# Drains on TensorE's queue behind its hand-overs in three stages of a graph network kernel

## The chip, the cores and the metric

The kernel runs on one core of a Trainium2 chip. A core has TensorE (matrix products into PSUM), VectorE, ScalarE, GpSimd and SyncE, each with an instruction queue of its own; they hand work to each other through semaphores, and DMA engines move data between HBM and the core's memories. The metric is the device time of one launch in microseconds. In the profile's rows PE is TensorE's matmuls, PEld its weight loads, PEldq its queue, DVE VectorE, ACT ScalarE, POOL GpSimd, SP SyncE.

## The reference

A graph has 3125 nodes with 32 features and 53125 edges, sorted by destination. Four layers follow each other, each on the normalised and rectified features, each added to them:

```python
h = maximum(layernorm(x), 0);  x = x + rel_layer(relu(rel_layer(h, V1, a1, ...)), V2, a2, ...)
h = maximum(layernorm(x), 0);  x = x + segment_sum(h[src], dst)                      # sum layer
h = maximum(layernorm(x), 0);  x = x + flow(h, edge_attr)                            # two edge MLPs, a node MLP
h = maximum(layernorm(x), 0);  x = attention(h) + x                                  # 4 heads of 8

def rel_layer(x, V, a, w_loop, bias):          # 20 edge types, 8 basis matrices
    W = einsum('rb,bio->rio', a, V)
    agg = segment_sum(x[src], dst * R + etypes).reshape(N, R, -1)
    return einsum('nri,rio->no', agg, W) + x @ w_loop + bias

def attention(x):
    scores = einsum('ehd,ehd->eh', q[dst], k[src]) * inv_sqrt_d
    e = exp(scores - segment_max(scores, dst)[dst])
    return (segment_sum(e[:, :, None] * v[src], dst) / segment_sum(e, dst)) @ Wo
```

## The kernel before

The edges are laid out in 440 tiles of 128, so that all edges of a tile have their destinations in one block of 128 nodes (25 blocks). A sum over the edges of a node is a matmul: the weights are a one-hot matrix of the tile's destinations (edges by nodes of the block), the moving operand is the tile's messages, and the result is added in PSUM to the block's columns. Which columns is data: TensorE reads the tiles' column offsets into registers first (`load_aligned`, line 84, and `load_columns`, line 1778).

The value of a source node comes to its edge in one of two ways. GpSimd gathers rows from a table in HBM, one indirect DMA for each tile (line 732 in the relational layers, 1038 in the sum layer, 1655 in attention). Or TensorE picks it from the node table that stands in SBUF: VectorE compares the tile's source numbers with the node numbers (`which`, lines 795 and 1073), and 25 matmuls, one for each block of nodes, add up the picked rows (lines 870 and 1126).

The stages follow each other; each is a block in which every engine has its own program, and the engines meet only through semaphores. The loops that concern us are written out in full, group after group. The order on TensorE is the order of the calls:

- Relational layers (two, 40 groups of 11 tiles each; 8 tiles gathered, 3 picked). For each group g: `pick(g)`, `gathered_messages(g)`, `coefficients(g)` (the type's 8 coefficients for the picked edges), `picked_messages(g-2)`, `basis_products(g)`. ScalarE takes the pick out of PSUM (line 844, waits for `pick_done`) and hands it back for the basis products; VectorE makes the one-hots (lines 782, 795, 804), weighs the basis products with the coefficients and adds them (812, 821). GpSimd may run 6 groups ahead and waits for `rows_used`, which `gathered_messages` gives.
- Sum layer (40 groups of 11 tiles, 7 gathered, 4 picked). For each group: `pick(g+1)`, `turn(g)` (transposes of the picked rows), `picked_rows(g-1)`, `gathered_rows(g)`. ScalarE copies between them (1100, 1104).
- Attention (55 groups of 8 tiles, in a pipeline of four steps). One step of TensorE has pieces of four groups: for tiles 0 to 3 `masked_scores`, each followed by two tiles of `pick_q` of the next group (and once by `pick_maxima` of the group before), for tiles 4 to 7 `masked_scores` with `turn_onehots` in between, then `add_up`, `turn_parts` and `load_columns`. VectorE takes each tile's maximum as its scores are done (1691), ScalarE turns and masks (1731, 1733, 1739).

Every such piece ends in the same way: the last matmul carries the update of the semaphore that another engine waits for, as in `pick` of the relational layers.

```python
for c in range(NB):
    last = pe.matmul(pp[g % 2][0:3 * F, 0:RW], hs[:, c].rearrange("p k f -> p (k f)"),
                     which[g % 2][:, c, :], start=(c == 0), stop=(c == NB - 1))
last.then_inc(pick_done, 1)
```

The flow stage between sum layer and attention, the sorting and the tables ahead of the layers are written likewise.

Of the kernel before, what the change touches and what calls it, by code (L numbers as in the profile page):

```python
# [679 lines left out]
def add_up_pass(nc, a, s, d, sb, ps, sem, k, init, finish):  # L680
# [4 lines left out]
    with ExitStack() as st:  # L685
        acc = ps(st, f"{name}_acc", [P, 2 * BANK])
        parts = init(st, acc)
        with ExitStack() as st1:
# [28 lines left out]
            with nc.Block() as block:  # L717
# [134 lines left out]
                def _(pe):  # L852
# [11 lines left out]
                    def pick(g):  # L864
                        load_aligned(pe, unused, regs[g % 3], s["dcol"][0:1, 0, :], g * RG)
                        pe.wait_ge(which_ready, g + 1)
                        if g >= 2:
                            pe.wait_ge(pick_taken, g - 1)
                        for c in range(NB):
                            last = pe.matmul(pp[g % 2][0:3 * F, 0:RW], hs[:, c].rearrange("p k f -> p (k f)"),  # L870
                                             which[g % 2][:, c, :], start=(c == 0), stop=(c == NB - 1))
                        last.then_inc(pick_done, 1)

                    def gathered_messages(g):
                        b = g % RBUFS
                        pe.wait_ge(hot_ready, g + 1)
                        pe.wait_ge(gathered[b], 16 * RGT * (g // RBUFS) + 16 * RGT)
                        for t in range(RGT):
                            last = add(g, t, rows[b][:, t, :])
                        last.then_inc(rows_used, 1)  # L880

                    def coefficients(g):
                        pe.wait_ge(kinds_ready, g + 1)
                        if g >= 1:
                            pe.wait_ge(coef_taken, g)
                        for t in range(RPT):
                            last = pe.matmul(pc[:, t * NBASIS:(t + 1) * NBASIS], kinds[g % 2][:, t * P:(t + 1) * P],
                                             ab[:], start=True, stop=True)
                        last.then_inc(coef_done, 1)

                    def basis_products(g):
# [3 lines left out]
                        for t in range(RPT):  # L895
                            for j in range(3):
                                last = pe.matmul(pz[:, t * NBASIS * F:(t + 1) * NBASIS * F],  # L897
                                                 gT[g % 2][:, t * P:(t + 1) * P], top(V[:])[:, j, :],
                                                 start=(j == 0), stop=(j == 2))
                        last.then_inc(z_done, 1)  # L900

                    def picked_messages(g):
                        pe.wait_ge(hot_ready, g + 1)
                        pe.wait_ge(msg_ready, g + 1)
                        for t in range(RPT):
                            last = add(g, RGT + t, msg[g % 2][:, t, :])
                        last.then_inc(used, 1)

                    for g in range(RGROUPS):
# [89 lines left out]
def sum_layer(nc, a, s, d, sb, ps, sem, more):  # L999
# [7 lines left out]
    with ExitStack() as st:  # L1007
# [5 lines left out]
        with ExitStack() as st2:  # L1013
# [16 lines left out]
            with nc.Block() as block:  # L1030
# [76 lines left out]
                def _(pe):  # L1107
# [12 lines left out]
                    def pick(g):  # L1120
# [4 lines left out]
                        for c in range(NB):  # L1125
                            last = pe.matmul(pp[g % 2][0:3 * F, 0:PT * P], hs[:, c].rearrange("p k f -> p (k f)"),  # L1126
                                             which[g % 2][:, c, :], start=(c == 0), stop=(c == NB - 1))
                        last.then_inc(pick_done, 1)

                    def gathered_rows(g):  # L1130
# [3 lines left out]
                        for t in range(GT):  # L1134
                            last = add(g, t, hot[b][:, t, :], [rows[b][:, t, :]])
                        last.then_inc(rows_used, 1)

                    def turn(g):
# [3 lines left out]
                        for t in range(PT):  # L1142
                            last = pe.transpose(pt[:, t * 3 * F:(t + 1) * 3 * F], turned[g % 2][:, t * P:(t + 1) * P],
                                                s["identb"][0:3 * F, 0:3 * F])
                        last.then_inc(turn_done, 1)

                    def picked_rows(g):
                        pe.wait_ge(hot_ready, g + 1)
                        pe.wait_ge(turn_taken, g + 1)
                        for t in range(PT):  # L1150
                            last = add(g, GT + t, hotb[g % bufs][:, t, :],
                                       [picked[g % 2][:, (3 * t + k) * F:(3 * t + k + 1) * F] for k in range(3)])
                        last.then_inc(used, 1)

                    groups = rounds * bufs
# [376 lines left out]
def attention_layer(nc, a, s, d, out, sb, ps, sem):  # L1532


    with ExitStack() as st:
# [81 lines left out]
        with ExitStack() as st2:  # L1617
# [29 lines left out]
            with nc.Block() as block:  # L1647
# [119 lines left out]
                def _(pe):  # L1767
                    regs = [pe.alloc_register(f"att_col{t}") for t in range(G)]

                    def turn_onehots(i, g, b):  # L1770
                        pe.wait_ge(hot_ready, g + 1)
                        for t in range(G):
                            last = pe.transpose(pOT[:, t * P:(t + 1) * P], hot[b][:, t, :], s["identb"][:])
                        last.then_inc(ot_done, 1)

                    def load_columns(i, g, b):
# [3 lines left out]
                    def pick_q(i, g, b, tiles):  # L1780
# [7 lines left out]
                        if tiles[-1] == G - 1:  # L1788
                            last.then_inc(q_done, 1)

                    def turn_parts(i, g, b):
                        pe.wait_ge(parts_ready, g + 1)
                        pe.sem_inc(go_pe, 1)
                        pe.transpose(pP[0:3 * G * HEADS, 0:P], top(sc[b][:].rearrange("p k t h -> p (k t h)")),
                                     s["identb"][:]).then_inc(parts_turned, 1)

                    def masked_scores(i, g, b, t):

                        if t == 0:
# [5 lines left out]
                        pe.matmul(r, pick[:, t, :], partT[b][:], start=False, stop=True, skip_group_check=True)\  # L1805
                            .then_inc(score_done, 1)

                    def pick_maxima(i, g, b):
                        pe.wait_ge(tparts_ready, g + 1)
                        pe.wait_ge(o_copied, g + 1)  # L1810
                        for t in range(G):
                            last = pe.matmul(pO[:, t * 3 * HEADS:(t + 1) * 3 * HEADS], OT[b][:, t, :],
                                             top(tm[b][:])[:, :, t, :], start=True, stop=True)
                        last.then_inc(rows_done, 1)

                    def add_up(i, g, b):
                        pe.wait_ge(mparts_ready, g + 1)
                        for t in range(G):
                            for k in range(3):
                                last = pe.matmul(pO[:, t * OW:(t + 1) * OW], hot[b][:, t, :], top(msg[b][:])[:, k, t, :],  # L1820
                                                 start=(k == 0), stop=(k == 2))
                        last.then_inc(o_done, 1)

                    pe.sem_inc(o_done, BUFS)
# [137 lines left out]
```

## Time and profile before

| | |
|---|---|
| median of 3 runs | 3510.46 us (3508.48 to 3511.75) |
| span of the profiled execution | 4186.2 us |
| mean granted clock of TensorE | 0.746 |
| busy share of the span: TensorE | 65% |
| VectorE | 63% |
| GpSimd | 56% |
| ScalarE | 13% |
| stages that the change touches (profiled) | relational 722 to 1240 and 1275 to 1800, sum 1830 to 2290, attention 3190 to 4095 us |
| flow stage (profiled) | 2330 to 3125 us |

The times in the rows are from one execution under the profiler, whose span is longer than the timed runs' median; the two are not mixed below without saying so. A matmul's end is modelled, its start is recorded. "Idle before" names what ended an engine's wait: another engine's line, "issue" where the profile shows nothing that it waited for, and "remote" where a semaphore update came that isn't traced to an instruction. The granted clock is a share of full speed.

### The profile page before, as it was taken

The numbers are of one execution on the slowest core, as the hardware profiler recorded it, in microseconds if no ns is written. First come the engines' busy times: TensorE is split into PE (matmuls) and PEld (weight loads), VectorE is DVE, ScalarE is ACT, GpSimd is POOL, SyncE is SP. The second block draws the span as 40 slices with busy tenths as digits, with TensorE's granted clock in tenths as the row PEclk, the third lists the DMA queues.
The fourth block names the chain that finished last, engine by engine and source line by source line (L and its number), as shares of the span: only waits on it lengthen the run. The fifth ranks groups of instructions, "written<-read, shape, count | busy, mean of one in ns | idle before, by whom it ended". The sixth has DMA issues, their size and how long they took to land. (4 is left out here: it accounts for less than half of the span.)

```text
span 4186.2 us, 55154 instructions
## 1 busy us (share of the span) xinstructions
PE 2723.7 (65%) x18509; PEld 1820.0 (43%) x18619; DVE 2656.6 (63%) x8007; ACT 533.4 (13%) x1242; POOL 2327.0 (56%) x2253
## 2 busy tenths in 40 slices
PE   0221001898895888957886899999994555555551
PEld 0100001676663676735554566666652222222221
DVE  9001002888854888868887688888854666665667
ACT  0000000000010000000100222222211222222220
POOL 3777774666606666446664566666725444444430
PEclk9555555777765777778887899999985667676665
DMA  5111002111111111111111000000000000000010
GB/s 88 39 37 26 7 7 62 21 21 21 19 62 38 21 22 22 13 22 23 24 24 16 10 10 10 11 10 11 11 4 21 16 17 17 17 17 16 18 14 4
DMA packets 125021, 91.49 MB, mean 22 GB/s; under 512 B 59542, under 2 KB 110678, under 8 KB 124118
## 3 DMA queue, kind: packets, MB, share of 16 engines
q0 software_dynamic: 70912, 41.10, 7.4%
q1 hardware_dynamic: 53846, 46.89, 4.7%
q8 instruction: 164, 2.69, 0.3%
q14 instruction: 99, 0.81, 0.1%
HBM read 60.42 MB, written 27.41 MB: 21 GB/s over the span
## 5 line engine op out<-in xcount | busy, mean ns | idle before, releaser
L732 POOL DMA_INDIRECT rel_rows<-message_table,message_indices x640 | 647.7, 1012 | 449.7 <-issue 173.8
L1287 POOL DMA_INDIRECT flow_x<-node_table,src_indices x440 | 524.9, 1193 | 293.4 <-PE p_x_turned L1406 153.7
L1655 POOL DMA_INDIRECT att_kv_rows<-kv_table,att_index x440 | 417.5, 949 | 474.4 <-DVE att_index L1666 342.7
L795 DVE TENSOR_SCALAR rel_source_onehot<-rel_sources,node_numbers 128x384 bf16<-128x384 f16 x2000 | 547.4, 321 | 208.3 <-remote 174.1
L393 POOL DMA_INDIRECT sorted_edges<-stage,sorted_row x416 | 429.6, 1033 | 191.7 <-issue 126.3
L1429 PE MATMUL flow_acc_bwd<-flow_onehot_j,flow_by_q 128*128 128x309 bf16 (+1 forms) x2530 | 516.9, 335 | 7.1 <-issue 0.2
L870 PE MATMUL p_rel_picked<-rel_source_onehot,rel_h_parts 128*96 128x384 bf16 x2000 | 458.4, 400 | 33.7 <-issue 24.6
L1691 DVE TENSOR_REDUCE att_tile_max<-p_att_scores 128x4 f32<-128x512 f32 x440 | 292.2, 688 | 236.6 <-PE p_att_scores L1805 166.9
L1038 POOL DMA_INDIRECT sum_rows<-node_table,src_indices x280 | 277.5, 991 | 220.5 <-issue 75.0
L870 PEld LDWEIGHTS p_rel_picked<-rel_source_onehot,rel_h_parts 128*96 128x96 bf16 x2000 | 309.2, 155 | 176.6 <-issue 33.3
L1073 DVE TENSOR_SCALAR sum_source_onehot<-sum_sources,node_numbers 128x512 bf16<-128x512 f16 x1000 | 309.1, 377 | 24.8 <-remote 24.8
L1803 PE MATMUL p_att_scores<-att_mask,identb 128*128 128x512 bf16 x440 | 235.6, 536 | 131.6 <-ACT att_parts_turned L1739 131.6
L1126 PE MATMUL p_sum_picked<-sum_source_onehot,sum_h_stack 128*96 128x512 bf16 x1000 | 271.5, 435 | 74.0 <-issue 51.6
L782 DVE TENSOR_TENSOR rel_onehot<-p_rel_lanes,dst_in_block 128x128 f32<-128x128 f32 x880 | 256.1, 291 | 15.7 <-issue 15.7
L1805 PE MATMUL p_att_scores<-att_parts_turned,att_pick 96*128 96x512 bf16 x440 | 241.7, 549 | 0.0
L1426 PE MATMUL flow_acc_fwd<-flow_messages,flow_onehot 128*128 128x32 bf16 x1320 | 235.4, 178 | 0.0
L624 PE MATMUL p_message<-w_rel,h_transposed 32*128 32x320 f32 x200 | 113.5, 744 | 186.8 <-issue 183.0
L1126 PEld LDWEIGHTS p_sum_picked<-sum_source_onehot,sum_h_stack 128*96 128x96 bf16 x1000 | 136.8, 141 | 195.2 <-issue 108.1
L601 DVE COPY message_rows<-p_message 128x320 f32<-128x320 f32 x50 | 24.6, 493 | 292.8 <-remote 227.0
L1341 DVE TENSOR_TENSOR flow_by_q<-flow_messages,source_q_mask 128x512 bf16<-128x512 bf16 x330 | 207.6, 684 | 0.0
L844 ACT CAST rel_picked<-p_rel_picked 96x384 bf16<-96x384 f32 x80 | 38.1, 476 | 1285.4 <-remote 851.6
L897 PE MATMUL p_rel_terms<-rel_basis_parts,rel_picked 96*128 96x256 bf16 x720 | 149.5, 378 | 74.4 <-issue 59.7
(287 smaller groups left out, 4502.7 us busy)
## 6 DMA issues: line engine op xcount, KB each, us to landing
message_table<-message_rows SPq DMA_DIRECT2D x50, 320.0 KB, 2.1
rel_rows<-message_table,message_indices POOLq DMA_INDIRECT x640
rel_sources<-source_rows SPq DMA_DIRECT2D x80, 96.0 KB
flow_x<-node_table,src_indices POOLq DMA_INDIRECT x440
att_kv_rows<-kv_table,att_index POOLq DMA_INDIRECT x440
sorted_edges<-stage,sorted_row POOLq DMA_INDIRECT x416
sum_sources<-source_rows SPq DMA_DIRECT2D x40, 128.0 KB
sum_rows<-node_table,src_indices POOLq DMA_INDIRECT x280
```

Of the source, the lines that this page charges most:

```text
L393: pool.indirect_dma_start(out=d["sorted"], out_offset=bass.IndirectOffsetOnAxis(ap=row[:, c:c + 1], axis=0), in_=stage[:, c, :], in_offset ...
L732: pool.indirect_dma_start(out=rows[b][:, t, :], out_offset=None, in_=d["messages"], in_offset=bass.IndirectOffsetOnAxis(ap=s["idx_msg"][:, ...
L782: last = dve.tensor_tensor(hot[b][:, lo:hi, :], lanes[:].unsqueeze(1).to_broadcast([P, hi - lo, P]), s["dstl"][:, g * RG + lo:g * RG + hi] ...
L795: last = dve.tensor_scalar(which[g % 2][:, c, :], srcs[b][:], s["node"][:, c:c + 1], None, ALU.is_equal)
L870: last = pe.matmul(pp[g % 2][0:3 * F, 0:RW], hs[:, c].rearrange("p k f -> p (k f)"), which[g % 2][:, c, :], start=(c == 0), stop=(c == NB ...
L1038: pool.indirect_dma_start(out=rows[b][:, t, :], out_offset=None, in_=d["nodes"], in_offset=bass.IndirectOffsetOnAxis(ap=s["idx_src"][:, g ...
L1073: last = dve.tensor_scalar(which[g % 2][:, c, :], srcs[g % bufs][:], node[:, c:c + 1], None, ALU.is_equal)
L1126: last = pe.matmul(pp[g % 2][0:3 * F, 0:PT * P], hs[:, c].rearrange("p k f -> p (k f)"), which[g % 2][:, c, :], start=(c == 0), stop=(c == ...
L1287: pool.indirect_dma_start(out=X[b][:, t, 0:F], out_offset=None, in_=d["nodes"], in_offset=bass.IndirectOffsetOnAxis(ap=s["idx_src"][:, g * ...
L1429: last = pe.matmul(accB[:, lo:hi], S[b][:, t, k, :], J[b][:, t, lo:hi], start=False, stop=True, skip_group_check=True)
L1655: pool.indirect_dma_start(out=KV[b][:, t, :], out_offset=None, in_=d["kv"], in_offset=bass.IndirectOffsetOnAxis(ap=ibuf[b][:, t:t + 1], ax ...
L1691: dve.tensor_reduce(tm[b][:, 0, t, :], pR[t % PR][:].rearrange("p (h e) -> p h e", h=HEADS), AX_X, ALU.max).then_inc(max_ready, 1)
```

## The change

A drain is put on TensorE's queue behind the instruction that carries a hand-over: in five functions of the relational layers, four of the sum layer and six of attention (in `pick_q` only behind the last tile of a group, in `masked_scores` behind each tile). The matmuls, their order, the semaphores and the waits stay, and so do the programs of the other engines. The flow stage, the tables and the ends of the stages are as before. A drain takes its place in the queue: nothing behind it starts before the array has finished what is ahead of it. On no engine does an instruction change its place among the others.

```diff
@@ pick, relational layers @@
                         last.then_inc(pick_done, 1)
+                        pe.drain()
...
@@ gathered_messages @@
                         last.then_inc(rows_used, 1)
+                        pe.drain()
...
@@ coefficients @@
                         last.then_inc(coef_done, 1)
+                        pe.drain()
...
@@ basis_products @@
                         last.then_inc(z_done, 1)
+                        pe.drain()
...
@@ picked_messages @@
                         last.then_inc(used, 1)
+                        pe.drain()
...
@@ pick, gathered_rows, turn, picked_rows of the sum layer, each alike @@
                         last.then_inc(turn_done, 1)
+                        pe.drain()
...
@@ turn_onehots @@
                         last.then_inc(ot_done, 1)
+                        pe.drain()
...
@@ pick_q @@
                         if tiles[-1] == G - 1:
                             last.then_inc(q_done, 1)
+                            pe.drain()
...
@@ turn_parts @@
                                      s["identb"][:]).then_inc(parts_turned, 1)
+                        pe.drain()
...
@@ masked_scores @@
                         pe.matmul(r, pick[:, t, :], partT[b][:], start=False, stop=True, skip_group_check=True)\
                             .then_inc(score_done, 1)
+                        pe.drain()
...
@@ pick_maxima @@
                         last.then_inc(rows_done, 1)
+                        pe.drain()
...
@@ add_up @@
                         last.then_inc(o_done, 1)
+                        pe.drain()
```

## Rows read from the trace of the kernel before

**Rows 1.** Busy time by stage: stretch, its us, busy us (instructions), clock, DMA, GB/s

```profile
722.00:1240.00 518.00, 463.25 (x2560) 355.77 (x2561) 403.67 (x1539) 28.28 (x93) 276.62 (x272) 0.76 0.14 25
...
1830.00:2290.00 460.00, 361.39 (x2221) 230.08 (x2222) 383.78 (x1178) 40.44 (x85) 274.15 (x278) 0.84 0.14 22
...
2330.00:3125.00 795.00, 785.56 (x6237) 519.55 (x6344) 632.22 (x1729) 205.16 (x429) 497.87 (x410) 0.99 0.07 10
...
3190.00:4095.00 905.00, 487.81 (x4415) 252.62 (x4415) 546.40 (x1527) 205.27 (x494) 404.78 (x427) 0.67 0.10 16
```

**Rows 2.** Waits of the whole span: engine, line, what for, total us, times, longest

```profile
ACT rel_picked L844 <- remote: 851.6, 69, 71.7
```

**Rows 3.** Timeline, relational group with GpSimd gathering: start, us, engine, line, operation [idle before]

```profile
1002.46 0.47 ACT L844 CAST rel_picked<-p_rel_picked 96x384 bf16<-96x384 f32 x1 [11.46 <-remote]
...
1004.89 5.74 PE L870 MATMUL p_rel_picked<-rel_source_onehot,rel_h_parts 128*96 128x384 bf16 x25
...
1012.21 0.95 POOL L732 DMA_INDIRECT rel_rows<-message_table,message_indices  x1 [0.30 <-issue]
...
1013.03 0.86 PE L861 MATMUL rel_acc<-rel_messages,rel_onehot 128*128 128x32 f32 x6
1014.46 0.47 ACT L844 CAST rel_picked<-p_rel_picked 96x384 bf16<-96x384 f32 x1 [11.44 <-remote]
```

**Rows 4.** Timeline, relational groups after GpSimd's last gather

```profile
1164.74 0.47 ACT L844 CAST rel_picked<-p_rel_picked 96x384 bf16<-96x384 f32 x1 [7.34 <-PE p_rel_picked L870]
...
1169.17 5.53 PE L870 MATMUL p_rel_picked<-rel_source_onehot,rel_h_parts 128*96 128x384 bf16 x25
...
1174.53 1.87 PE L861 MATMUL rel_acc<-rel_rows,rel_onehot 128*128 128x32 f32 x16
1174.73 0.47 ACT L844 CAST rel_picked<-p_rel_picked 96x384 bf16<-96x384 f32 x1 [7.35 <-PE p_rel_picked L870]
...
1176.01 0.40 DVE L804 TENSOR_SCALAR rel_type_onehot<-rel_types,lane_number 20x384 f32<-20x384 f16 x1
...
1176.33 0.83 PE L887 MATMUL p_rel_coef<-rel_type_coef,rel_type_onehot 20*128 20x8 f32 x6
...
1177.78 1.36 PE L897 MATMUL p_rel_terms<-rel_basis_parts,rel_picked 96*128 96x256 bf16 x9
...
1178.95 5.76 PE L870 MATMUL p_rel_picked<-rel_source_onehot,rel_h_parts 128*96 128x384 bf16 x25
```

**Rows 5.** Busy time of one such group, columns as in rows 1

```profile
1164.00:1174.00 10.00, 10.00 (x64) 8.03 (x63) 10.00 (x40) 0.65 (x2) 0.00 (x0) 0.83 0.01 2
```

**Rows 6.** Timeline of TensorE in attention

```profile
3503.52 1.03 PE L1773 MATMUL p_att_onehot<-identb,att_onehot 128*128 128x128 bf16 x8 [1.70 <-issue]
...
3513.37 0.61 PE L1803 MATMUL p_att_scores<-att_mask,identb 128*128 128x512 bf16 x1 [2.78 <-ACT att_parts_turned L1739]
...
3524.73 1.03 PE L1773 MATMUL p_att_onehot<-identb,att_onehot 128*128 128x128 bf16 x8 [6.33 <-DVE att_onehot L1671]
...
3537.11 0.95 PE L1773 MATMUL p_att_onehot<-identb,att_onehot 128*128 128x128 bf16 x8 [2.23 <-issue]
```

**Rows 7.** Line 717, block end: TensorE queue's drains, min/median/max ns, first and last start

```profile
L717 PEldq DRAIN  x2: 3518/3540/3562, 1200.9 to 1799.4; - x2
```

**Rows 8.** Timeline ahead of the first of these drains' ends

```profile
1200.81 3.60 PE L861 MATMUL rel_acc<-rel_rows,rel_onehot 128*128 128x32 f32 x16
```

**Rows 9.** Line 861, gathered messages: columns as in rows 7

```profile
L861 PEld LDWEIGHTS rel_acc<-rel_rows,rel_onehot x1280: 190/192/333, 735.1 to 1802.4; 128*128 128x128 f32 x183
L861 PE MATMUL rel_acc<-rel_rows,rel_onehot x1280: 192/276/419, 735.3 to 1802.5; 128*128 128x32 f32 x183
```

**Rows 10.** Line 84, the picks' register load: columns as in rows 7

```profile
L84 PEldq TENSOR_LOAD <-dst_columns x120: 851/1211/1508, 707.5 to 2250.5; - x120
```

**Rows 11.** Timeline of TensorE's picked rows at the sum layer's end

```profile
2249.69 0.46 PE L1116 MATMUL sum_acc<-sum_picked,sum_onehot_bf 128*128 128x32 bf16 x12
...
2257.67 0.46 PE L1116 MATMUL sum_acc<-sum_picked,sum_onehot_bf 128*128 128x32 bf16 x12
```

More of the change, by code:

```diff
@@ L1806, in masked_scores @@
                             .then_inc(score_done, 1)
+                        pe.drain()
                     def pick_maxima(i, g, b):
@@ L1814, in pick_maxima @@
                         last.then_inc(rows_done, 1)
+                        pe.drain()
                     def add_up(i, g, b):
@@ L1822, in add_up @@
                         last.then_inc(o_done, 1)
+                        pe.drain()
                     pe.sem_inc(o_done, BUFS)
```

## The prediction

> **What bounds the kernel now.** I read the table of stages first, then the waits, then the timelines of one group of each changed stage, and last the rows from which a drain can be priced. Of the stages that the change touches, the first relational layer takes 518 us (the second is its twin, 80 groups in the two), the sum layer 460 us (40 groups) and attention 905 us (55 groups). The flow stage of 795 us is not touched: TensorE is busy in 785.56 of it [rows 1].
>
> In the touched stages no engine is full on average, and the list of waits says why: ScalarE waits 851.6 us in 69 pieces for the relational pick by the name "remote" [rows 2]. The timeline of one group shows the piece. The pick starts at 1004.89 and takes 5.74 us, so it ends at 1010.63. ScalarE, which waits for nothing but its hand-over, starts at 1014.46, which is 3.83 us later. Until just before, GpSimd had been issuing gathers, the last of the bunch at 1012.21 for 0.95 us. TensorE itself had gone on in between, up to 1013.89. So the update that the matmul carries came late, 1.30 us after GpSimd's bunch had ended. One group lasts 12.0 us in this state (ScalarE at 1002.46 and at 1014.46) [rows 3].
>
> Once GpSimd has nothing left to gather, the hand-over is prompt: the pick that starts at 1169.17 for 5.53 us ends at 1174.70, and ScalarE starts at 1174.73. A group then lasts 9.99 us (1164.74 to 1174.73) [rows 4], with TensorE and VectorE both busy in 10.00 of 10.00 us at a granted clock of 0.83, a mix of the two levels, 1.2 and 2.4 GHz [rows 5]. In that prompt state VectorE and TensorE hold each other: the coefficients start at 1176.33, when the type one-hot of VectorE (1176.01, 0.40 us) has ended, and all else on TensorE is back to back [rows 4].
>
> Attention has both states next to each other. From one turn of the one-hots to the next it is 21.21 us (3503.52 to 3524.73) and then 12.38 us (to 3537.11). In the long step TensorE waits 6.33 us for one-hots [rows 6]. The mean step is 905/55 = 16.5 us.
>
> **Which state do the timed runs have?** The profiled execution spans 4186.2 us, and the median of the timed runs is 3510.46, so 676 us belong to the profiling or to what it provokes. Flow can't give them, since TensorE fills it. If the late updates were absent from timed runs, the groups would save (12.0 − 10.0) × 80 = 160 us, (16.5 − 12.4) × 55 = 225 us and, down to VectorE's own 383.78/40 = 9.6 us a group instead of 460/40 = 11.5, 1.9 × 40 = 76 us: together 461 of the 676. I take it that timed runs are mostly in the prompt state, at some 3 to 1. It is an inference from sizes: a GpSimd that issues faster without the profiler could explain a part as well. I work out the change in the prompt state, against the profile's span (4186.2 + the sum), and put the same difference on the median.
>
> **The change, part by part.** It removes nothing and moves no matmul, no wait and no DMA. It adds 5 drains a group in the relational layers (400), 4 in the sum layer (160), 13 in attention (715): 1275. Each stands on TensorE's own queue behind an instruction that already carries the hand-over, so what is queued behind it is TensorE's next piece, and who waits for that is VectorE or ScalarE.
>
> *Price of one drain.* The trace has some at block ends. One starts at 1200.9 and lasts 3562 ns, to 1204.46 [rows 7]; the matmuls that it waits for end at 1200.81 + 3.60 = 1204.41 [rows 8]. So it ends 0.05 us behind the last matmul. What it breaks is the overlap: one 128x32 matmul takes 276 ns and its weight load 192 ns [rows 9], while 16 of them take 1.87 us, 0.117 each [rows 4]. So the last matmul's end costs 276 − 117 = 0.16 us, and the next weight load, no longer ahead, 0.1 to 0.19. That makes 0.05 + 0.16 + 0.14 = 0.35 us where TensorE would have gone straight on. The lower end is 0.05 or nothing, where a wait follows that ends later anyway. The upper end, with the slowest of these forms, is 419 − 117 + 333 = 635 ns [rows 9]. I take 0.35, since it comes from the median row.
>
> *The register load.* The pick of the relational and the sum layer begins with a load of eleven or so columns: 851 to 1508 ns, median 1211 [rows 10]. It doesn't occupy the array, and today it runs while earlier matmuls do: a pick of the prompt state starts at 1178.95, just as the basis products end (1177.78 + 1.36 = 1179.14) [rows 4], with no hole of 1.2 us between. With a drain ahead of it, the array is empty during it. So it costs up to 1.2 us a group, and nothing if TensorE would wait for one-hots meanwhile.
>
> *Relational layers.* 5 × 0.35 + 1.2 = 2.95 us of added TensorE time a group. TensorE's work at full clock is at most 10.0 × 0.83 = 8.3 us, so if the clock rose to full it would be 11.25 against VectorE's 10.0, +1.25; if it stays at 0.83, +2.95. Late next is the coefficients' hand-over, then VectorE's weighing. I take +1.8, nearer the lower end, for VectorE's queue has whole one-hots to do meanwhile: 1.8 × 80 = 144 us. Bounds: 0 (drains of 0.05, load beside the wait for one-hots) and 5 × 0.635 + 1.5 = 4.7, so 0 to 374 us.
>
> *Sum layer.* At the layer's end, where VectorE has no one-hots left to make, a group takes TensorE 2249.69 to 2257.67, 8.0 us [rows 11]. The added 4 × 0.35 + 1.2 = 2.6 us give 10.6 against VectorE's 9.6: +1.0 × 40 = 40 us. Bounds: 0, and with drains of 0.635 and a load of 1.5, 12.0 against 9.6, so 98 us.
>
> *Attention.* Of 13 drains, those behind the second four tiles are covered: VectorE's queue has them one behind the other. The one behind the turned parts is covered by the wait for ScalarE, 2.78 us in the step shown [rows 6]. In the first half of a step the picks of q stand between the tiles and TensorE sets the pace, so those four count, with the maxima, the one-hots and the sums: 7 × 0.35 = 2.45, less some slack, as VectorE is busy 546.40/55 = 9.9 us of a prompt step's 12.4 [rows 1, 6]. I take 2.0 × 55 = 110 us; bounds 0 and 13 × 0.35 = 4.5, so 250 us.
>
> Sum: 144 + 40 + 110 = +294 us, so 4480 against the profile's span and 3804 against the median, which I round to 3800; the bounds together are 0 and +722.
>
> **A page against the change.** By the row, an update came 3.83 us after the end of its matmul in one state and 0.03 us after in the other [rows 3, 4]. The Trainium skill ("PSUM — Partial Sum Buffer", section "Engine vs sequencer instructions") says that an update attached to the producing instruction fires when that completes, and that a drain waits for the engine to be fully idle. By that rule there is no late update for a drain to release, and the gain side of the sum is zero; rows 4 agree with it and rows 3 don't.
>
> **Rivals.**
> *Late updates are real and a drain lets them out (faster).* Place: the pick's hand-over to ScalarE and the scores' to VectorE, in the state of rows 3 and of the long step of rows 6. Then the relational group goes from 12.0 to 11.25 (its TensorE work with drains), the sum group from 11.5 to 10.6, the attention step from 16.5 to 12.4 + 2.0 = 14.4: −60 − 36 − 115 = −211, so 3300 us. It decides once a held update costs more than the drains, 2.95 us in a relational group and 2 in a step. For it: the update comes in the traced groups only after GpSimd pauses. Against it: the 676 us, and that TensorE was already waiting with nothing left to do in part of these gaps, as a drain would make it, and the update still hadn't come (1013.89 to 1014.46) [rows 3].
> *Late updates are real, and the drain waits for them too (slower).* TensorE would stand from 1010.63 to 1014.46 instead of working 3.2 us: up to 3.2 × 80 = 256, and in the other two stages hardly less per group than the drains there cost anyway, 150: about 3920.
> *Hidden (same).* VectorE is full in 10.00 of 10.00 us [rows 5]; if the drains cost 0.05 and the clock rises a little, nothing moves: 3510.
> *The clock falls (much slower).* In attention, where TensorE is busy half of the time, the granted clock is 0.67, and in flow, where it never stops, 0.99 [rows 1]. Were the relational layers to fall from 0.83 to 0.67, their 8.3 us would be 12.4 and the group 12.4 + 2.95 = 15.35: +5.35 × 80 = 428, with the rest 578, so 4088. The Trainium skill ("TensorE: Matmul & The Clock Gate", section "A second HAM failure mode: psum-queue depth-cycling") tells of a kernel whose short idles between groups of matmuls made the clock swing; rows 1 fit that and do not prove it.
>
> **How the numbers follow.** My forecast 0.55; released updates 0.20; hidden 0.10; the clock 0.10; drains that wait 0.05. A measurement of this kernel can't tell less than about 0.2% (7 us) from no change. Faster is the release alone, 0.20; same is the hidden case, 0.10; slower is the rest, 0.70. The forecast's own range is 3600 to 3950. The range of 8 in 10 reaches down into the release, to 3400 (two thirds of that case lie below), and up to 3990, which leaves half of the clock's case out.
>
> **What would show it.** Right: drains of some 0.05 us behind the last matmul in the trace, a hole of about 1.2 us on TensorE ahead of each relational pick, relational groups at GpSimd's end of 11 to 12.5 us instead of 10.0, attention's short steps of 14 instead of 12.4, flow unchanged. Wrong: ScalarE's waits by the name "remote" gone and the median below 3503 (updates released); groups still of 10.0 us at the relational layer's end (hidden); a granted clock near 0.67 there (the clock).

## The result and the profile after

The changed kernel took 4364.78 us (4 runs, 4363.09 to 4368.16), the kernel before 3509.47 beside it: a ratio of 1.2445, 95% interval 1.243 to 1.246, or +855 us. The forecast was 3800, in a range up to 3990. The direction was right, the size was off by almost a factor of three.

The late hand-overs of rows 2 and 3 are not there any more. In the list of waits ScalarE now waits for the pick itself in all 80 groups:

```profile
ACT rel_picked L844 <- PE p_rel_picked L870: 1374.0, 80, 500.7
```

But they are not there in the kernel before either, when it is profiled once more (the first experiment below). So the comparison is made against that second profile. Period by period, ScalarE's take-out of the pick in the first relational layer gives (first and last start of 40) after and before:

```profile
L844 ACT CAST rel_picked<-p_rel_picked x40: 474/474/476, 659.7 to 1220.1; 96x384 bf16<-96x384 f32 x40
```

```profile
L844 ACT CAST rel_picked<-p_rel_picked x40: 475/475/476, 658.0 to 1047.4; 96x384 bf16<-96x384 f32 x40
```

That is 560.4/39 = 14.37 us a group against 389.4/39 = 9.98. In the sum layer, after and before:

```profile
L1109 ACT COPY sum_picked<-p_sum_turned x40: 478/478/479, 1931.7 to 2428.6; 128x384 bf16<-128x384 bf16 x40
```

```profile
L1104 ACT COPY sum_picked<-p_sum_turned x40: 479/479/481, 1597.7 to 1938.4; 128x384 bf16<-128x384 bf16 x40
```

12.74 against 8.74 us. In attention, 55 steps, after and before:

```profile
L1754 ACT ACTIVATE att_messages<-att_gap x55: 229/229/230, 3355.1 to 4265.7; 128x32 f32<-128x32 f32 x55
```

```profile
L1745 ACT ACTIVATE att_messages<-att_gap x55: 229/229/230, 2853.1 to 3404.4; 128x32 f32<-128x32 f32 x55
```

16.86 against 10.21 us. So +4.39 x 80 + 4.00 x 40 + 6.65 x 55 = 351 + 160 + 366 = 877, about the 855 that were timed.

The busy times of the stages answer to [rows 1]. After (columns as there: stretch, its us, busy us of PE, PEld, DVE, ACT, POOL, then the granted clock):

```profile
700.00:1190.00 490.00, 403.30 (x2089) 288.38 (x2089) 340.49 (x1319) 21.72 (x67) 258.32 (x262) 0.73 0.11 16
1960.00:2400.00 440.00, 363.25 (x1856) 216.10 (x1856) 292.83 (x975) 32.57 (x68) 237.61 (x239) 0.76 0.12 19
2470.00:3240.00 770.00, 768.57 (x6246) 511.03 (x6247) 622.88 (x1722) 204.66 (x432) 618.95 (x426) 0.99 0.07 10
3400.00:4200.00 800.00, 646.86 (x3778) 249.05 (x3777) 462.40 (x1312) 175.97 (x417) 353.93 (x374) 0.50 0.09 16
```

Before, in the second profile:

```profile
700.00:1000.00 300.00, 296.15 (x1873) 238.84 (x1872) 300.00 (x1171) 19.80 (x61) 230.84 (x228) 0.85 0.15 25
1620.00:1920.00 300.00, 278.18 (x1863) 182.89 (x1862) 300.00 (x980) 32.62 (x68) 228.10 (x237) 0.93 0.15 28
2880.00:3380.00 500.00, 351.04 (x3961) 193.92 (x3959) 464.70 (x1369) 189.35 (x437) 380.56 (x393) 0.88 0.14 27
```

Two things are to be seen. VectorE filled the relational and the sum stage before (300 of 300 us), with TensorE at 296 and 278, so there was nearly no slack to put a drain into. And the granted clock, a share of full speed, is lower: 0.85 to 0.73, 0.93 to 0.76, 0.88 to 0.50. Flow, with no drains, stays at 0.99. Below, full and half clock are the two levels, 2.4 and 1.2 GHz; a granted clock between 0.50 and 1 is a mix of them.

One relational group after, on TensorE and ScalarE, answers to [rows 4] (line numbers differ a little from kernel to kernel, by the lines added):

```profile
1002.53 1.97 PE L861 MATMUL rel_acc<-rel_rows,rel_onehot 128*128 128x32 f32 x16 [0.32 <-issue]
...
1004.72 0.80 PE L889 MATMUL p_rel_coef<-rel_type_coef,rel_type_onehot 20*128 20x8 f32 x6 [0.22 <-issue]
...
1005.83 0.98 PE L861 MATMUL rel_acc<-rel_messages,rel_onehot 128*128 128x32 f32 x6 [0.31 <-issue]
...
1007.02 2.08 PE L900 MATMUL p_rel_terms<-rel_basis_parts,rel_picked 96*128 96x256 bf16 x9 [0.21 <-issue]
...
1010.72 7.15 PE L870 MATMUL p_rel_picked<-rel_source_onehot,rel_h_parts 128*96 128x384 bf16 x25 [1.62 <-DVE rel_source_onehot L795]
...
1017.91 0.47 ACT L844 CAST rel_picked<-p_rel_picked 96x384 bf16<-96x384 f32 x1 [12.18 <-PE p_rel_picked L870]
```

The holes are 0.32 + 0.22 + 0.31 + 0.21 + 1.62 = 2.68 us a group. The last is named after VectorE, but on TensorE's queue the drain behind the basis products and then the register load fill it (queue instructions, ns and start):

```profile
L904 PEldq DRAIN  x1: 2083/2083/2083, 1007.1 to 1007.1; - x1
```

```profile
L84 PEldq TENSOR_LOAD <-dst_columns x1: 1342/1342/1342, 1009.2 to 1009.2; - x1
```

The drain starts at 1007.065 and ends at 1009.15, 0.05 us behind the matmuls of 1007.02 + 2.08, and the load runs from 1009.2 for 1.34 us; the pick starts at 1010.72.

### The profile page after: what moved, and what is told of

It reads as the page before. It is cut to its first block and busy times, and to the rows that moved or that the text cites. A ratio compares the mean times of both kernels' runs of the same rounds, so it can differ in the third digit from the quotient of the medians.

```text
span 4366.3 us, 56539 instructions
## 1 busy us (share of the span) xinstructions
PE 3147.2 (72%) x18619; PEld 1899.1 (43%) x18619; DVE 2632.6 (60%) x8007; ACT 541.8 (12%) x1242; POOL 2396.0 (55%) x2253
## 5 line engine op out<-in xcount | busy, mean ns | idle before, releaser
L1296 POOL DMA_INDIRECT flow_x<-node_table,src_indices x440 | 633.4, 1439 | 186.6 <-issue 133.8
L870 PE MATMUL p_rel_picked<-rel_source_onehot,rel_h_parts 128*96 128x384 bf16 x2000 | 512.1, 436 | 111.7 <-DVE rel_source_onehot L795 57.8
L1438 PE MATMUL flow_acc_bwd<-flow_onehot_j,flow_by_q 128*128 128x512 bf16 x2640 | 540.4, 336 | 0.0
L393 POOL DMA_INDIRECT sorted_edges<-stage,sorted_row x416 | 405.5, 975 | 192.0 <-issue 126.5
L870 PEld LDWEIGHTS p_rel_picked<-rel_source_onehot,rel_h_parts 128*96 128x96 bf16 x2000 | 328.3, 169 | 303.2 <-DVE rel_source_onehot L795 74.2
L1131 PE MATMUL p_sum_picked<-sum_source_onehot,sum_h_stack 128*96 128x512 bf16 x1000 | 312.5, 487 | 64.2 <-issue 54.0
L1815 PE MATMUL p_att_scores<-att_mask,identb 128*128 128x512 bf16 x440 | 263.8, 600 | 91.0 <-ACT att_parts_turned L1748 67.1
L1817 PE MATMUL p_att_scores<-att_parts_turned,att_pick 96*128 96x512 bf16 x440 | 279.0, 634 | 0.0
L1796 PEld LDWEIGHTS p_att_rows<-att_q_parts,att_onehot_turned 128*128 128x128 bf16 x1320 | 137.3, 104 | 241.0 <-issue 209.8
L1796 PE MATMUL p_att_rows<-att_q_parts,att_onehot_turned 128*128 x1320 | 192.3, 205 | 56.1 <-issue 51.9
```

Of the source, the lines that this page charges most:

```text
L393: pool.indirect_dma_start(out=d["sorted"], out_offset=bass.IndirectOffsetOnAxis(ap=row[:, c:c + 1], axis=0), in_=stage[:, c, :], in_offset ...
L1296: pool.indirect_dma_start(out=X[b][:, t, 0:F], out_offset=None, in_=d["nodes"], in_offset=bass.IndirectOffsetOnAxis(ap=s["idx_src"][:, g * ...
L1438: last = pe.matmul(accB[:, lo:hi], S[b][:, t, k, :], J[b][:, t, lo:hi], start=False, stop=True, skip_group_check=True)
L1796: last = pe.matmul(pQ[:, t * F:(t + 1) * F], OT[b][:, t, :], top(q[:])[:, k, bass.ds(c, F)], start=(k == 0), stop=(k == 2))
```

## The experiments

The reasons that were weighed: A, a drain costs what TensorE's queue can no longer do beside earlier matmuls (overlap, register steps, the register load), and a clock that falls with the holes; B, one price for each drain, 855/1275 = 0.67 us; later D, the eight drains behind attention's scores count alike.

**The kernel before, profiled again** (no edit).

> The kernel before, profiled once more. In the runs with drains in one stage alone, the stages without drains showed no late updates and the profiled span was within 2 us of the timed median. Theory A (the late updates were a matter of that one profiled execution, or of profiling a program with no drain in it, and were never in the timed runs): timed at 3507 in any case; the span is either near 3510 with relational groups of 10.0 and attention steps of 10.2 us (that one execution), or again near 4186 (profiling this program). Theory C (late updates are part of the kernel's own time): span near 4186 and a timed run that agrees with it, which the median already speaks against.

Timed 3506.91, and:

```profile
span 3505.1 us, 55264 instructions
```

```profile
ACT rel_picked L844 <- PE p_rel_picked L870: 1101.7, 80, 499.3
```

The late updates and the 676 us belonged to that one profiled execution, not to the kernel and not to profiling it. What put that execution into this state isn't settled. GpSimd's gathers in the relational layers took as long in both (1.01 us each), so slower gathers were not it.

**Each stage alone.**

```diff
 rel_only:  pe.drain() behind pick, gathered_messages, coefficients, basis_products, picked_messages
 sum_only:  pe.drain() behind pick, gathered_rows, turn, picked_rows
 att_only:  pe.drain() in the six functions of attention
```

> The drains of the two relational layers alone, 400 of 1275. Theory A (a drain costs what the queue no longer does ahead: overlap of matmuls, register steps and the load ahead of the pick, and the clock that falls with the holes): the relational groups of the changed kernel take 585/40 = 14.6 us against 10.0 in the prompt state, so +370 us, about 3880; span of the profile still some hundred us over the timed median, since sum and attention are as before. Theory B (one price for each drain wherever it stands, 855/1275 = 0.67 us): +268, 3778. My forecast's own term: +144, 3654.

> The drains of the sum layer alone, 160 of 1275. Theory A: 518/40 = 12.95 us a group against 9.6, +134 us, about 3644. Theory B: +107, 3617. My forecast's own term: +40, 3550.

> The drains of attention alone, 715 of 1275. Theory A: 936/55 = 17.0 us a step against 12.4 or a little less, +253 to +350 us, 3763 to 3860; clock there 0.50 in the trace. Theory B: +480, 3990. My forecast's own term: +110, 3620.

3839.46, 3661.45 and 3877.94 against 3506.67: ratios 1.0946 [1.0928, 1.0964], 1.0442 [1.0424, 1.0459] and 1.1057 [1.1038, 1.1075], or +333, +155 and +371. They add up to +859, the whole change. For each drain that is 0.83, 0.97 and 0.52 us, so B falls: the price depends on the place. Attention's +371 is above A's +253 to +350, too.

**Where in the relational group.**

```diff
 rel_basis_only:   only
                         last.then_inc(z_done, 1)
+                        pe.drain()
 rel_load_ahead:   all five, and in basis_products
                         last.then_inc(z_done, 1)
+                        if g + 1 < RGROUPS:
+                            load_aligned(pe, unused, regs[(g + 1) % 3], s["dcol"][0:1, 0, :], (g + 1) * RG)
                         pe.drain()
                   and in pick the load stays for the first group only
+                        if g == 0:
                             load_aligned(pe, unused, regs[g % 3], s["dcol"][0:1, 0, :], g * RG)
```

> One drain a group, behind the basis products, ahead of the register load of the next pick: 80 of the 400. Theory A (holes plus the clock that falls with them, no slack on TensorE, which is busy 297 of 300 us in this stage without drains): a hole of 1.2 to 1.6 us and as much again at most for the clock, +100 to +200 us, 3607 to 3707. Theory B (0.67 us for each drain): +54, 3561. My forecast's view (1.2 us of load, slack of 1.7 us against it): 0 to +30.

> All five relational drains, 400, but the register load of the next pick issued behind the basis products and ahead of their drain, so that it runs beside them. Against the five drains with the load behind (+333): Theory A: the hole of 1.1 to 1.6 us ahead of the pick falls to 0.3, so at least 80 x 1.0 = 80 us less, 120 to 160 less if the clock comes back with it: +170 to +250. If the load is not what fills that hole: +333 as before.

One drain of the five, the one ahead of the load, costs +136 us (1.0386 [1.0368, 1.0403]), 1.70 us a group. With all five and the load moved ahead of the drain it is +219 (1.0625 [1.0608, 1.0643]) instead of +333: 114 us less, 1.43 a group. The hole ahead of the pick went from 1.62 to 0.21 us, by the basis products and the pick of that run:

```profile
918.20 2.08 PE L901 MATMUL p_rel_terms<-rel_basis_parts,rel_picked 96*128 96x256 bf16 x9 [0.21 <-issue]
920.49 6.13 PE L871 MATMUL p_rel_picked<-rel_source_onehot,rel_h_parts 128*96 128x384 bf16 x25 [0.21 <-issue]
```

So the load, with the clock that came back (0.73 to 0.76), is a third of what the relational drains cost.

**Attention: which drains.**

```diff
 att_scores_only:  pe.drain() behind each masked score (440)
 att_first_half:   the same with  if t < G // 2:   (220)
 att_second_half:  the same with  if t >= G // 2:  (220)
 att_parts_only:   pe.drain() behind turn_parts only (55)
 att_behind_q:     none behind scores, but at the end of every pick_q (220)
```

> Of attention's drains only the eight behind the masked scores, 440. Theory A: in the first half of a step the picks of q that follow have register steps of 0.12 us each that no longer run ahead, about 0.9 us a drain, in the second half a quarter of that or nothing: (4 x 0.9 + 0 to 1) x 55 = 200 to 250 us, 3710 to 3760, most of what all 13 cost. Theory B: 440 x 0.67 = 295, 3805. If the clock alone does it (any break lets it fall to 0.50): nearly the same as with all 13.

> Drains behind the masked scores of tiles 0 to 3 alone, 220. Behind each stands pick_q, whose matmuls have an address from a register: in the drained trace they start 0.12 us apart, 0.74 for six, where without drains TensorE's queue makes these steps while the scores run (0.80 us from one tile to the next in all). Theory A: at full clock a tile then takes 0.43 + 0.25 + 0.74 = 1.42 instead of 0.80, four of them 2.5 us a step, and up to 1.2 more as the clock falls: +137 to +200 us, 3645 to 3708. Theory D (all eight drains of the scores count alike): half of +265, 3640.

> Drains behind the masked scores of tiles 4 to 7 alone, 220. What follows has fixed addresses. Theory A: 0.27 us each at full clock (0.71 instead of 0.44 from tile to tile), VectorE's reductions at 0.62 us a tile cover most of it; with some loss of clock 0 to 1.2 us a step, 0 to +66 us, 3508 to 3575. Theory D: half of +265, 3640. My forecast had these four at nothing.

> One drain a step, behind the turned parts, 55: TensorE waits there for ScalarE anyway, 1.2 us in the undrained trace; the register load of the next columns (0.59 us) now starts behind the drain, within that wait. Theory A and my forecast: nothing, 3508 within 7 us. Theory B (0.67 us a drain): +37, 3545.

> As many drains as in the run with the first half's scores alone (220, four a step), but each behind the pick_q that follows the score, ahead of the next score, whose addresses are fixed. The register steps of pick_q run again beside the scores. Theory A (the steps that no longer run ahead make most of the price): 0.25 to 0.4 us a drain in place of 0.82, and less loss of clock: +40 to +100 us, 3550 to 3610. If the drain costs by the break as such, wherever it stands in the half: +181 as before, 3690.

| | time, us | ratio, 95% interval | us more |
|---|---|---|---|
| eight behind scores | 3771.92 | 1.0752 [1.0734, 1.077] | +265 |
| first four | 3691.90 | 1.0516 [1.0499, 1.0534] | +181 |
| last four | 3514.67 | 1.0013 [1.0004, 1.0023] | +3 |
| behind the turned parts | 3509.12 | 0.9993 [0.9984, 1.0003] | −2 |
| four a step behind pick_q | 3567.04 | 1.0164 [1.0147, 1.0181] | +58 |

D falls: of two times four drains the first cost 0.82 us each and the others, alone, next to nothing. Two things tell them apart: what stands behind a drain, and whether TensorE has a wait to take it. The same number a step as in the first half, put behind pick_q instead of ahead of it, costs 0.26 us each; between those tiles there is no wait, so what stands behind decides. The timeline shows why. Before, from one masked score to the next in the first half it takes 1.02 us at half clock (3104.27 to 3105.29) and 0.82 at full (3114.37 to 3115.19):

```profile
3104.27 0.59 PE L1803 MATMUL p_att_scores<-att_mask,identb 128*128 128x512 bf16 x1
...
3105.08 0.36 PE L1786 MATMUL p_att_rows<-att_q_parts,att_onehot_turned 128*128 x6
3105.29 0.59 PE L1803 MATMUL p_att_scores<-att_mask,identb 128*128 128x512 bf16 x1
...
3114.37 0.38 PE L1803 MATMUL p_att_scores<-att_mask,identb 128*128 128x512 bf16 x1
...
3114.81 0.54 PE L1786 MATMUL p_att_rows<-att_q_parts,att_onehot_turned 128*128 x6
3115.19 0.38 PE L1803 MATMUL p_att_scores<-att_mask,identb 128*128 128x512 bf16 x1
```

After, at half clock too, it takes 1.95 us (3605.92 to 3607.87), with pick_q behind the score and not beside it:

```profile
3605.92 0.59 PE L1815 MATMUL p_att_scores<-att_mask,identb 128*128 128x512 bf16 x1
3606.30 0.63 PE L1817 MATMUL p_att_scores<-att_parts_turned,att_pick 96*128 96x512 bf16 x1
3607.16 0.86 PE L1796 MATMUL p_att_rows<-att_q_parts,att_onehot_turned 128*128 x6 [0.23 <-issue]
3607.87 0.59 PE L1815 MATMUL p_att_scores<-att_mask,identb 128*128 128x512 bf16 x1
```

The six matmuls of pick_q read their addresses from registers. Their queue has a register step ahead of each (four of 46 ns on line 1796, two of 68 on line 1794), and they start 0.12 to 0.15 us apart, from 3605.1 to 3605.9 (a pick_q of the changed kernel: matmuls, and the steps on line 1796):

```profile
L1796 PE MATMUL p_att_rows<-att_q_parts,att_onehot_turned x6: 203/206/207, 3605.1 to 3605.9; 128*128 x6
L1796 PEldq FUSED_REGOPS  x4: 46/46/46, 3605.2 to 3605.8; - x4
```

It is not the array or the loading of weights that sets this pace. At the same half clock the same six take 0.36 us without a drain ahead (3105.08) and 0.86 with it, and the eight matmuls of pick_maxima, with weights of the same size but fixed addresses, take 0.36 right behind a drain:

```profile
3611.05 0.36 PE L1825 MATMUL p_att_sums<-att_tile_max,att_onehot_turned 128*128 128x12 bf16 x8 [0.21 <-issue]
```

Without a drain the queue makes these steps while the score runs. At full clock the scores are short, the steps follow each other without a break, and the 0.82 us of a tile are about their pace: pick_q is slower there (0.54 us) than at half clock. With the drain moved behind pick_q they run beside the score again, 1.03 us from score to score at full clock:

```profile
3010.43 0.39 PE L1804 MATMUL p_att_scores<-att_mask,identb 128*128 128x512 bf16 x1 [1.22 <-ACT att_parts_turned L1739]
...
3011.46 0.39 PE L1804 MATMUL p_att_scores<-att_mask,identb 128*128 128x512 bf16 x1
```

The last four drains are free only while there is a wait to take them. The first four and the last four cost 181 and 3, but all eight 265, 81 more than the two together (A had forecast 200 to 250). Before, TensorE waits 1.29 us for the one-hots of the second half; with the first four drains in (att_first_half) it arrives later and at half clock, and this wait is gone. The granted clock fell a little more as well, from 0.62 with four drains to 0.58 with eight, and how the 81 us split between the two isn't shown.

```profile
3109.44 0.62 PE L1773 MATMUL p_att_onehot<-identb,att_onehot 128*128 128x128 bf16 x8 [1.29 <-DVE att_onehot L1671]
```

```profile
3009.18 1.06 PE L1773 MATMUL p_att_onehot<-identb,att_onehot 128*128 128x128 bf16 x8
```

The other five drains of a step make the 106 us from 265 to att_only's 371; of these only the one behind the turned parts was run alone.

**A wait in the drain's place.**

```diff
 att_own_wait:
                             .then_inc(score_done, 1)
+                        pe.wait_ge(score_done, g * G + t + 1)
```

> No drain at all: TensorE waits, behind each masked score, for the semaphore update that this very matmul sends. The queue stands still for as long as with a drain. Theory A (it is the standing still that costs): as with the eight drains, +265 us or a little more, 3770 to 3830. If the drain instruction itself has a price: clearly less, below 3700.

3741.96, ratio 1.0654 [1.0637, 1.0672], +231 where eight drains cost +265. That lies between the two forecasts, nearer to A's: most of the price is the standing still of the queue, and a drain costs 34/440 = 0.08 us more than such a wait. The hole ahead of pick_q is 0.17 us in this run, 0.23 with a drain:

```profile
3005.50 0.88 PE L1786 MATMUL p_att_rows<-att_q_parts,att_onehot_turned 128*128 x6 [0.17 <-PE p_att_scores L1805]
```

**Does the clock come back with more work?**

```diff
 att_more_work: all 13 drains, and in masked_scores
+                        for _ in range(3):
                             pe.matmul(r, s["identb"][:], away[b]..., start=True, stop=False, ...)
 rel_more_work: all five drains, and in pick
+                        for c in range(8):
+                            pe.matmul(pp[g % 2]..., hs[:, c]..., which[g % 2][:, c, :], start=True, stop=True)
                         for c in range(NB):
```

> All 13 attention drains, and the first matmul of each masked score done three times over (it starts its accumulation anew, so the scores are the same): 16 matmuls of 512 columns a step for nothing. If attention's granted clock stays at 0.50: they take 0.43 us each, 6.9 us a step, +378 us on top of +371, about 4256. If the longer unbroken work brings the clock near full: they take 0.22 each, 3.5 us, but the 13.6 us of busy time falls to about 7.2, so the step is 14 instead of 16.9 us, about 3717, faster than without the useless work. That would show that the clock is the larger part of what attention's drains cost.

> All five relational drains, and ahead of each pick eight of its matmuls done once for nothing (each closed at once, then the pick starts anew): 0.16 us each at full clock, 0.33 at half. If the clock of this stage stays at 0.74 of full: 8 x 0.22 = 1.75 us a group, +140 on top of +333, about 3980. If the longer unbroken work brings the clock back, the pick's own 25 matmuls take 4.2 us instead of 5.8 to 7.2 and pay for part of it: +20 to +80 on top, 3860 to 3920.

Attention: 4062.46, 1.1579 [1.1559, 1.1598], +553, so 182 us on top of att_only's +371, between the two numbers. 3.3 us a step were added by matmuls that would take 6.9 at half clock and 3.5 at full, and the granted clock rose from 0.50 to 0.68:

```profile
2880.00:3880.00 1000.00, 839.43 (x4737) 337.08 (x4735) 483.88 (x1371) 185.49 (x441) 366.86 (x390) 0.68 0.06 14
```

What a drained tile takes at either level stands next to each other in the run with the first four drains alone: from score to score 1.51 us at full clock (3000.45 to 3001.96) and 1.96 at half (3003.48 to 3005.44):

```profile
3000.45 0.39 PE L1803 MATMUL p_att_scores<-att_mask,identb 128*128 128x512 bf16 x1 [1.22 <-ACT att_parts_turned L1739]
...
3001.96 0.38 PE L1803 MATMUL p_att_scores<-att_mask,identb 128*128 128x512 bf16 x1
...
3003.48 0.59 PE L1803 MATMUL p_att_scores<-att_mask,identb 128*128 128x512 bf16 x1
...
3005.44 0.59 PE L1803 MATMUL p_att_scores<-att_mask,identb 128*128 128x512 bf16 x1
```

Undrained it is 0.82 and 1.02. So of the 1.13 us by which a tile grew (0.82 at full to 1.95 at half clock), some 0.7 are there at full clock, and some 0.4 are the clock's. My claim that the clock is the larger part in attention does not hold for these tiles.

Relational: 3998.29, 1.1397 [1.1378, 1.1416], +489, 156 on top of the five drains: 1.95 us a group for eight matmuls, no less than the 1.75 forecast for an unchanged clock, and the clock did not come back (0.74 in rel_only):

```profile
700.00:1190.00 490.00, 416.21 (x2089) 300.83 (x2087) 297.42 (x1161) 19.59 (x60) 247.54 (x250) 0.71 0.10 16
```

So more work lifted the clock in attention and not here. Which holes decide on it stays open.

None of the versions is faster than the kernel before.

## Why the prediction was wrong in size

**Right: no release.** The timed runs were in the prompt state, as I took from the 676 us, and there was no late update that a drain could let out. The reading as to why went too far: it was neither the profiler as such nor a GpSimd that issues faster, but a state of that one execution. The Trainium skill's sentence in "PSUM — Partial Sum Buffer" ("Engine vs sequencer instructions"), that the update fires when the instruction completes, agrees with the later profiles: in the second one of the kernel before and in the changed kernel's, ScalarE starts 0.04 us behind the pick's modelled end in all 80 groups.

**Right: the drain's own end, the load and the covered ones.** The added drains of the changed kernel end 0.05 us behind the last matmul's modelled end (0.09 in one of 1275). The load behind the drain cost 1.43 us a group, some of it by the clock (forecast 1.2). The last four tiles and the turned parts cost nothing, as forecast, when theirs are the only drains; with the first four drained the last four cost another 81 us, and the trace shows that the wait that covered them is gone.

**Relational, forecast +1.8 us a group, measured +4.4.** The added time was sized well: 2.95 us forecast, 2.68 in holes. The step that failed is the slack that I took off it, up to 1.7 us by letting the clock rise to full; it fell instead. TensorE's busy time went from 296.15/300 x 9.98 = 9.85 to 403.30/490 x 14.37 = 11.83 us a group, while busy time times clock stayed (9.85 x 0.85 = 8.4, 11.83 x 0.73 = 8.6). So the clock fell and added 2.0 us. It shows in the pieces. Before, basis products (line 897) and pick (870) take 1.19 and 4.23 us in one group and 2.08 and 6.24 in the next, at the higher and partly the lower level; after, in the group above, 2.08 and 7.15:

```profile
801.01 1.19 PE L897 MATMUL p_rel_terms<-rel_basis_parts,rel_picked 96*128 96x256 bf16 x9
802.03 4.23 PE L870 MATMUL p_rel_picked<-rel_source_onehot,rel_h_parts 128*96 128x384 bf16 x25
...
808.65 0.98 PE L861 MATMUL rel_acc<-rel_messages,rel_onehot 128*128 128x32 f32 x6
810.10 2.08 PE L897 MATMUL p_rel_terms<-rel_basis_parts,rel_picked 96*128 96x256 bf16 x9 [0.47 <-DVE rel_terms L812]
811.98 6.24 PE L870 MATMUL p_rel_picked<-rel_source_onehot,rel_h_parts 128*96 128x384 bf16 x25
```

This was the rival "the clock falls", at +5.35 a group and a chance of 0.10; it should have been part of the forecast, because the granted clock fell in all three stages that got holes. The Trainium skill tells of a kernel whose short idles between groups of matmuls made the clock swing between its two levels ("TensorE: Matmul & The Clock Gate", "A second HAM failure mode: psum-queue depth-cycling"). The 0.73 and 0.76 of the relational and the sum layer, between the levels, agree; attention's 0.50 is no swing but the lower level throughout.

**Sum, forecast +1.0, measured +4.0.** Base and slack were wrong. I took 9.6 us a group from a profile in the disturbed state [rows 1]; the group takes 8.74 and VectorE fills it. With 8.74 the same working gives 8.0 + 2.6 − 8.74 = +1.9; the rest goes with the clock that was left out. Idle time on TensorE rose from 0.64 to 2.2 us a group (21.82/300 x 8.74, 76.75/440 x 12.74), and busy time from 8.1 to 10.5, with the clock at 0.76 instead of 0.93.

**Attention, forecast +2.0, measured +6.65.** Base again: 12.4 from the shortest step of the disturbed profile [rows 6], 10.21 in truth, so the slack beside VectorE's 9.9 us was hardly there. The step that failed most is the price: 0.35 us a drain counted the overlap of two matmuls and left out the queue's register steps, which by the rows of attention take six times 0.12 to 0.15 us for a pick_q. At full clock alone that makes 0.7 us for each of the four tiles; with the clock's part, 1.13 us each, they make 4.5 of the 6.65. The cover that I gave the last four drains held only as long as the wait behind them.

Together, as an estimate by idle and busy time in the relational and the sum layer and by the tiles of the first half in attention: of the 877 us some 410 are holes and steps in series (2.4 us x 80, 1.6 x 40, 2.8 x 55), some 350 the lower clock (2.0 x 80, 2.4 x 40, 1.7 x 55). Attention's remaining 2.1 us a step, some 117 us, aren't split between the two by any run, so which of them is the larger in the whole stays open.

## What to carry to other kernels

A drain, or a wait for one's own result, is paid for by what stands behind it on the queue. In this kernel, with what the clock added, it was nothing where a longer wait follows and as long as that wait is there, 0.26 us ahead of matmuls with fixed addresses, 0.8 ahead of matmuls whose addresses come from registers, 1.7 ahead of a register load. Prices of single drains did not add up: 181 + 3 became 265. Where holes go with a lower clock, as they did here, a hole's price is more than its length, and slack that a higher clock would give must not be counted on. And a profile whose span is a fifth longer than the timed median is taken again before anything is read from it.

## What the runs showed of the hardware

- One execution of the same program ran with late semaphore updates of TensorE (3.8 us in the group of [rows 3]) and 676 us longer; none of the fifteen other profiles here did. The cause is open.
- In attention TensorE was busy in 646.86 of 800 us at a granted clock of 0.50, so all at the lower of its two levels, while before it was busy in 351.04 of 500 us at 0.88. The larger busy share (81% against 70%) went with the lower clock; a part of it is the lower clock's own doing.
- The six matmuls with addresses from registers took 0.36 us where the queue had made their register steps beforehand, and 0.86 behind a drain, at the same half clock. Eight with fixed addresses took 0.36 behind a drain.
